# Turning the k product of a fused adaLN block from fp32 into three fp32r products

## The reference, cut to what matters

```python
x_prev = jnp.concatenate([jnp.zeros((B, 1, C), x.dtype), x[:, :-1, :]], axis=1)
xr = mu_r * x + (1.0 - mu_r) * x_prev
xk = mu_k * x + (1.0 - mu_k) * x_prev
r = jax.nn.sigmoid(jnp.einsum('btc,dc->btd', xr, W_r))
k = jnp.einsum('btc,dc->btd', xk, W_k)
k_act = jnp.square(jax.nn.relu(k))
out = r * jnp.einsum('btc,dc->btd', k_act, W_v)
```

## Time and profile before

| | |
|---|---|
| median of 3 runs | 732.72 us (731.6 to 733.01) |
| the profiled execution | 733.41 us |
| its span | 731.8 us, 11552 instructions |
| TensorE clock, mean granted | 0.979 |
| busy: TensorE, VectorE, ScalarE, GpSimd | 679.8, 524.3, 392.5, 387.3 us |
| the k product (L1274 into `work`) | 236 records of 592 ns, 106.2 us busy |
| the last product (L1108, L1109, L1110) | 78.1, 70.6, 70.7 us busy |

### The profile page before, as it was taken

One profiled execution on the slowest core, in us unless ns is written; L12 is line 12 of the kernel. 1 busy time (PEld: TensorE's weight loads), 2 busy tenths in 40 slices (PEclk: granted clock), 3 DMA queues, 4 the chain that ended last, 5 costly groups with the idle time before them and its releaser, 6 DMA issues. The chain is left out here.

```text
span 731.8 us, 11552 instructions
## 1 busy us (share of the span) xinstructions
PE 679.8 (93%) x3554; PEld 546.8 (75%) x3554; DVE 524.3 (72%) x1030; ACT 392.5 (54%) x871; POOL 387.3 (53%) x809
## 2 busy tenths in 40 slices
PE   5972999999999999999999999999999999998496
PEld 2751777888878777888878787888868787886475
DVE  4571699786877688786877688786877687477453
ACT  0330566554755656554755666555755566545453
POOL 4224487757635762757635762757535772255230
PEclk9996899999999999999999999999999999999899
DMA  8329536564764849463854848463854557424425
GB/s 300 102 75 239 162 123 153 93 146 121 161 135 74 205 86 208 79 152 106 180 114 78 202 93 201 85 154 98 183 111 79 115 99 166 86 61 84 58 29 87
DMA packets 90968, 93.02 MB, mean 127 GB/s; under 512 B 4216, under 2 KB 88992, under 8 KB 90944
## 3 DMA queue, kind: packets, MB, share of 16 engines
q0 software_dynamic: 33264, 33.03, 30.6%
q1 hardware_dynamic: 55600, 57.02, 24.9%
q10 hardware_dynamic: 2080, 2.68, 1.1%
HBM read 42.84 MB, written 33.10 MB: 104 GB/s over the span
## 5 line engine op out<-in xcount | busy, mean ns | idle before, releaser
L1224 PE MATMUL att<-m_sb,z_t 128*128 128x256 f32 x496 | 114.6, 385 | 19.9 <-issue 12.9
L1224 PEld LDWEIGHTS att<-m_sb,z_t 128*128 128x128 f32 x496 | 93.6, 192 | 37.0 <-issue 25.2
L1257 PE MATMUL work<-w_r_t,mx 128*128 128x256 f32 x464 | 105.2, 380 | 1.6 <-DVE mx L892 1.6
L1274 PE MATMUL work<-mx,w_k_t 128*128 128x512 f32 x236 | 106.2, 592 | 0.0
L863 DVE SCALAR_TENSOR_TENSOR t_buf<-att,rs_o,g_row 128x256 f32<-128x256 f32 x124 | 51.4, 477 | 65.7 <-POOL rs_o L467 65.6
L676 ACT ACTIVATE z<-x,ag 128x256 f32<-128x256 f32 x128 | 66.5, 597 | 56.0 <-POOL ag L460 56.0
L1257 PEld LDWEIGHTS work<-w_r_t,mx 128*128 128x128 f32 x464 | 85.9, 190 | 12.7 <-DVE mx L892 1.9
L629 ACT ACTIVATE sq<-att 128x256 f32<-128x256 f32 x124 | 46.0, 382 | 86.8 <-PE att L1224 86.8
L438 POOL TENSOR_TENSOR ag<-st 128x4 f32<-128x4 f32 x32 | 19.5, 610 | 134.6 <-DVE st L874 134.6
L1206 PE MATMUL gram<-z 128*128 128x256 f32 (+1 forms) x512 | 89.1, 327 | 0.0
L1206 PEld LDWEIGHTS gram<-z 128*128 128x128 f32 x512 | 79.8, 191 | 6.6
(11 more groups left out here) (169 smaller groups left out, 1362.1 us busy)
## 6 DMA issues: line engine op xcount, KB each, us to landing
x_in<-in_L_attn_x_dram SPq DMA_DIRECT2D x32, 512.0 KB, 5.3
x<-rows SPq DMA_DIRECT2D x32, 512.0 KB, 3.5
x<-in_L_attn_x_dram POOLq DMA_DIRECT2D x32, 512.0 KB, 9.4
out_dram<-x SPq DMA_DIRECT2D x31, 512.0 KB, 4.8
out_dram<-y POOLq DMA_DIRECT2D x29, 512.0 KB, 6.0
rows<-row_scratch SPq DMA_DIRECT2D x16, 128.0 KB, 3.5
rows<-row_scratch SPq DMA_DIRECT2D x8, 256.0 KB, 3.9
wqkv_sb<-in_L_attn_w_qkv_dram ACTq DMA_DIRECT2D x1, 1536.0 KB, 10.8
```

Source lines behind the costliest of these rows:

```text
L1224: ins = mm(att_banks(j, alone)[q][:, (t % 2) * D:(t % 2 + 1) * D], z_t[:, j, k, t * P:(t + 1) * P], m_sb[:, k], start=(k == 0), stop=(k == ...
L1257: ins = mm(r_banks(alone)[q][:, (t % 2) * D:(t % 2 + 1) * D], mixed(j, alone)[0][:, ch, tile], w_r_t[:, ch], start=(ch == 0), stop=(ch == ...
L1274: ins = mm(k_banks(alone)[dh][:], w_k_t[:, ch, rows_dh], mixed(j, alone)[1][:, ch], start=(ch == 0), stop=(ch == KD - 1))
```

## The change

`ffn_k` goes from one fp32 product to `mm3`, three fp32r products of high and low parts, with 512 columns each. The weights are kept as `w_k_hi` and `w_k_lo`: ScalarE's copy writes the high part, and `split_k` on VectorE the low part, once before row 0. For each chunk ScalarE copies `xk` into `xk_hi` (`split_xk`, 128x1024) and VectorE subtracts it from `xk` into `xk_lo` (`low_xk`, 128x1024). Both are single buffers and wait until the product before has been done. `ffn_k` waits for `xk_lo_ready` in place of `xk_mixed`, and `mix` waits for `xk_lo_ready` of the chunk before in place of `k_done`. `low_xk` of a chunk stands behind another operation on VectorE: behind `gate_o` of the chunk before for chunks 0 and 1, behind `stats_2` for chunk 2 and behind `stats_a` for chunk 3. The diff, cut:

```diff
@@ -92,7 +92,8 @@
         bv_col = sb("bv_col", [P, NP])
         wfc_c = sb("wfc_c", [P, NP, D])
         w_r_t = sb("w_r_t", [P, KD, D])
-        w_k_t = sb("w_k_t", [P, KD, D])
+        w_k_hi = part("w_k_hi", [P, KD, D])
+        w_k_lo = part("w_k_lo", [P, KD, D])
         w_v_t = sb("w_v_t", [P, KD, D])
         mu_col = sb("mu_col", [P, 2, KD])
         wv_t = sb("wv_t", [P, NP, D])
...
@@ -638,6 +643,12 @@
                     nc.scalar.activation(h2t[:, h, 1 + j * CT:1 + (j + 1) * CT], tr[h][:], ACT.Identity,
                                          bias=mod_now[:, h:h + 1], scale=mod_now[:, 2 + h:3 + h]).then_inc(h2_ready, 1)
+            def split_xk(b, j, alone=False):
+                i = CH * b + j
+                wait_past(act, k_done, 2 * i)
+                act.wait_ge(xk_mixed, i + 1)
+                nc.scalar.activation(xk_hi[:], mixed(j, alone)[1], ACT.Copy).then_inc(xk_hi_ready, 1)
+
             def take_r(b, j, alone=False):
                 i, y_j = CH * b + j, y_buf(j, alone)
...
@@ -681,6 +692,8 @@
                 n = b + 1
                 squares(b, 0)
+                if not first:
+                    split_xk(b - 1, 3)
                 copy_z_t(n, 0)
                 prep_base_qk(n)
                 if first:
...
@@ -696,6 +709,7 @@
                 copy_h2(b, 0)
                 squares(b, 2)
                 copy_z_t(n, 2)
+                split_xk(b, 0)
                 take_r(b, 0)
                 make_z2(b, 1)
                 take_k(b, 0)
...
@@ -703,11 +717,13 @@
                 squares(b, 3)
                 make_z2(b, 2)
                 copy_z_t(n, 3)
+                split_xk(b, 1)
                 copy_gram(n)
                 copy_gram_low(n)
                 copy_h2(b, 2)
                 take_r(b, 1)
                 take_k(b, 1)
+                split_xk(b, 2)
                 copy_gq(n)
                 make_z2(b, 3)
                 exps(n)
...
@@ -728,17 +745,21 @@
                 make_z2(b, 1)
                 squares(b, 3, alone=True)
                 copy_h2(b, 1)
+                split_xk(b, 0)
                 take_r(b, 0)
                 make_z2(b, 2)
                 take_k(b, 0, halves=(0,))
                 take_k(b, 0, halves=(1,))
+                split_xk(b, 1)
                 copy_h2(b, 2)
                 take_r(b, 1, alone=True)
                 make_z2(b, 3)
                 take_k(b, 1, alone=True)
+                split_xk(b, 2, alone=True)
                 copy_h2(b, 3)
                 take_r(b, 2, alone=True)
                 take_k(b, 2, alone=True)
+                split_xk(b, 3, alone=True)
                 take_r(b, 3, alone=True)
                 take_k(b, 3, alone=True)
...
@@ -755,7 +776,7 @@
             copy_gram_low(0)
             copy_gq(0)
             exps(0)
-            copy_weights(2, [(w_r_t[:], work[0]), (w_k_t[:], work[1]), (w_v_t[:], work[2])])
+            copy_weights(2, [(w_r_t[:], work[0]), (w_k_hi[:], work[1]), (w_v_t[:], work[2])])
             copy_pv(0)
             row_steps(0, True)
             with act.Fori(1, B - 1) as b:
...
@@ -879,7 +900,7 @@
                 i = CH * b + j
                 if not alone:
                     wait_past(dve, r_done, 2 * i - 2)
-                    wait_past(dve, k_done, 2 * i - 2)
+                    wait_past(dve, xk_lo_ready, i - 1)
                 wait_past(dve, xk_mixed, i)
                 dve.wait_ge(x2_ready, CH * b + (min(j + 2, CH) if made is None else made))
...
@@ -892,6 +913,12 @@
                         ins = nc.vector.scalar_tensor_tensor(dst[:, h], dif[:, h], mu_col[:, n, h:h + 1], prev[:, h],
                                                              ALU.mult, ALU.add)
                     ins.then_inc(ready, 1)
+
+            def low_xk(b, j, alone=False):
+                i = CH * b + j
+                dve.wait_ge(xk_hi_ready, i + 1)
+                wait_past(dve, k_done, 2 * i)
+                nc.vector.tensor_tensor(xk_lo[:], mixed(j, alone)[1], xk_hi[:].bitcast(F32), ALU.subtract).then_inc(xk_lo_ready, 1)
             def low_k(b, j, alone=False):
                 i = CH * b + j
...
@@ -951,6 +978,13 @@
                     ins = nc.vector.scalar_tensor_tensor(res[0:n, k], last_c[0:n], neg_d[0:n], res[0:n, k],
                                                          ALU.mult, ALU.add)
                 ins.then_inc(qk_ready, 1)
+
+            def split_k():
+
+                dve.wait_ge(w_copied, 4)
+                nc.vector.tensor_tensor(w_k_lo[:].rearrange("p k d -> p (k d)"), work[1][:],
+                                        w_k_hi[:].rearrange("p k d -> p (k d)").bitcast(F32),
+                                        ALU.subtract).then_inc(w_split, 1)
             def softmax_dif(b):
                 dve.wait_ge(score_done, b + 1)
...
@@ -1008,6 +1042,7 @@
                     prep_qk(n)
                 else:
                     gate_o(b - 1, 3)
+                low_xk(b, 0)
                 take_wvf(b)
                 make_x2(b, 2)
                 stats_2(b, 2)
...
@@ -1015,10 +1050,12 @@
                 make_z(n, 3)
                 mix(b, 1)
                 gate_o(b, 0)
+                low_xk(b, 1)
                 make_x2(b, 3)
                 mix(b, 2)
                 low_k(b, 1)
                 stats_2(b, 3)
+                low_xk(b, 2)
                 if far:
                     stats_a(n + 1, 0)
                 gate_o(b, 1)
...
@@ -1035,6 +1072,7 @@
                 mix(b, 3)
                 if far:
                     stats_a(n + 1, 3)
+                low_xk(b, 3)
                 gate_o(b, 2)
             def last_row(b):
...
@@ -1047,18 +1085,22 @@
                 make_x2(b, 2, mixes=0, alone=True)
                 mix(b, 0, made=3)
                 gate_o(b - 1, 3)
+                low_xk(b, 0)
                 stats_2(b, 2)
                 mix(b, 1, made=3)
                 make_x2(b, 3, mixes=2, alone=True)
                 take_wvf(b, alone=True)
                 low_k(b, 0)
+                low_xk(b, 1)
                 stats_2(b, 3)
                 mix(b, 2, alone=True)
                 gate_o(b, 0)
                 low_k(b, 1, alone=True)
+                low_xk(b, 2, alone=True)
                 mix(b, 3, alone=True)
                 gate_o(b, 1, alone=True)
                 low_k(b, 2, alone=True)
+                low_xk(b, 3, alone=True)
                 low_k(b, 3, alone=True)
                 gate_o(b, 2, alone=True)
                 gate_o(b, 3, alone=True, add=True)
...
@@ -1090,6 +1132,7 @@
             make_z(1, 0)
             make_z(1, 1)
             dve.wait_ge(mod_col_ready, 2)
+            split_k()
             dve.wait_ge(w_copied, 5)
             row_steps(0, True, True)
             with dve.Fori(1, B - 2) as b:
...
@@ -1261,7 +1304,7 @@
             def ffn_k(b, j, alone=False):
                 i = CH * b + j
-                pe.wait_ge(xk_mixed, i + 1)
+                pe.wait_ge(xk_lo_ready, i + 1)
                 for dh in range(KD):
                     if dh == 0 and not alone:
                         wait_past(pe, ro_ready, 2 * i)
...
@@ -1271,8 +1314,9 @@
                         pe.wait_ge(k_lo_ready, 2 * i - 1 + dh)
                     rows_dh = slice(dh * P, (dh + 1) * P)
                     for ch in range(KD):
-                        ins = mm(k_banks(alone)[dh][:], w_k_t[:, ch, rows_dh], mixed(j, alone)[1][:, ch],
-                                 start=(ch == 0), stop=(ch == KD - 1))
+                        ins = mm3(k_banks(alone)[dh][:],
+                                  (w_k_hi[:, ch, rows_dh], w_k_lo[:, ch, rows_dh], xk_hi[:, ch], xk_lo[:, ch]),
+                                  start=(ch == 0), stop=(ch == KD - 1))
                     ins.then_inc(k_done, 1)
             def ffn_out(b, j, alone=False):
...
@@ -1413,6 +1457,7 @@
             pe.wait_ge(fc_ready, 1)
             make_m(0)
             pe.wait_ge(w_copied, 5)
+            pe.wait_ge(w_split, 1)
             row_steps(0, True)
             with pe.Fori(1, B - 1) as b:
                 row_steps(b, False)
```

More of the change, by code:

```diff
@@ L148, in adaln_block @@
         xr, xk = mx[:, 0], mx[:, 1]
+        xk_hi, xk_lo = (part(n, [P, KD, CT]) for n in ("xk_hi", "xk_lo"))
         k_hi, k_lo = (part(n, [P, 2, KD, CT]) for n in ("k_hi", "k_lo"))
@@ L211, in adaln_block @@
         w_copied = sem("w_copied")
+        w_split = sem("w_split")
         row8_stored = sem("row8_stored")
@@ L265, in adaln_block @@
         xr_mixed = sem("xr_mixed")
+        xk_hi_ready = sem("xk_hi_ready")
+        xk_lo_ready = sem("xk_lo_ready")
         k_done = sem("k_done")
```

## The result

The changed kernel takes **740.4 us** (median of 4 runs, 739.43 to 741.02) against 732.35 us for the kernel before, run beside it (4 runs): ratio 1.0109, interval 1.0092 to 1.0127. It is 1.1% slower. 728.7 was forecast, and the range ended at 736.5.

The account below looks back on a forecast made before the run. The prediction took a steady row as bound by TensorE's program order with one wait, for `t_buf`. Six rows -8.4, row 0 0 and last row +4.3 gave -4.1, about 728.7 us from a 732.72 median; range 723.0 to 736.5.

Parts of the forecast that it names:

- The start: Before row 0, split_k's 0.7 us on VectorE lies hidden in 2.2 us of waiting for a row DMA: 0.
- the bodies: Steady rows from attention 2 to the next attention 0, with products 0, 1 and 2: 2.3 us shorter each.
- The product: Each chunk's k product: twelve passes at 0.216 us, 2.6 us in place of 3.44, 0.85 less.
- a rival (12%): Passes of the k product take 0.238 us: 0.27 less gain in each of 18 body products, 733.9 us, no change; 12%.
- More than 0.23 apart: Sign of being wrong: the k product's passes stand more than 0.23 us apart, where 0.216 was forecast.
- a cost of each instruction: Reading of the fp32r product's extra 0.011 us: 256 columns don't quite cover it, 512 do, hence 0.216 a pass.
- The seam: Steady rows from attention 0 to attention 2, with the row before's product 3: 0.9 us longer.
- three waits as described: Seam: VectorE stands some 2 us for ScalarE's copy, its 2.47 idle is used up, attention 2 waits 1.8 for t_buf.
- The fourth: Seam: TensorE waits 1.0 us for k_lo ahead of ffn_out(3).
- Row 0: The first row: chunk 1 comes 0.6 to 1.4 late, product 2 gives 0.85 back; net 0, ends -1 and +1.
- The last row: Row 7: +4.3 us; make_x2(0) 2.2 late, subtractions ahead of statistics +1.2 and +1.1, partly offset by shorter products.
- The rival on the slower side: The seam costs 2.2 us in ordinary rows too, by GpSimd stretched beside two-input VectorE operations: 736.5 us; 18%.

Follow-up runs that it names:

- e1: The changed kernel without TensorE's wait for the weights' low part (w_split) ahead of row 0: 735.59 us, ratio 1.0037.
- e5: The changed kernel with all its added VectorE and ScalarE work, but the k product left in fp32: 752.35 us, ratio 1.0256.
- e2: The changed kernel with chunk 3's subtraction low_xk behind gate_o of chunk 2 in the steady rows: 733.92 us, ratio 1.0012.
- e6: The kernel before with only the new fp32r product, fed by parts made once: 721.6 us, ratio 0.9831.
- e3: The changed kernel with ScalarE's copy split_xk of chunk 3 ahead of the next row's first squares, last row included: 738.0 us, ratio 1.006.
- e11: The changed kernel with only chunk 1's last-row subtraction moved, ahead of making x of chunk 3: 740.26 us, ratio 1.0094.
- e10: The changed kernel with split_k right behind softmax_norm(0), low_xk(b,3) behind gate_o, and both last-row subtractions moved into VectorE's idle places: 730.3 us, ratio 0.9929.
- e4: The changed kernel with the last row's subtractions of chunks 0 and 1 behind the statistics of chunks 2 and 3: 739.02 us, ratio 1.0084.
- e9: The changed kernel with the last row's subtractions of chunks 0 and 1 both behind the mix of chunk 1: 740.18 us, ratio 1.0086.

## Why the prediction was wrong

**The start: the step that failed.** "`split_k` (0.7) lies in 2.2 us of waiting for a row DMA: 0." I priced it in VectorE's queue and found it hidden there, which is true. I didn't ask who waits for it. The diff's last line has TensorE wait for it ahead of all of row 0, and VectorE reaches it only behind two chunks of the next row's normalization. The cost is 4.45 us (e1: gone with the line). With it added, -4.1 becomes about 0 and the sign is lost; 733.2 would still have been inside the range, and it took the bodies' 3.3 and the smaller terms below to leave it. The text costed the wait for the activations' low part wherever it stands, and this one nowhere.

**The product: right in kind, mis-sized.** 0.216 a pass was taken and 0.233 measured, near the 0.238 that I had as the bound and as a rival (12%). "More than 0.23 apart" was one of the signs of being wrong, and it came. The reading "a cost of each instruction" was a guess between two rows that could not tell; 0.119 at 256 columns fits a cost of each column as well. 1.75 a body in place of 2.3 is 3.3 us over six rows. The rival's sum, 733.9, is right about the steady rows (81.38 measured, 82.05 - 1.4 + 0.8 = 81.45 by it), but partly by luck: it takes 0.27 off product 0 as well, whose gain the prediction had already cut to 0.6, and has the seam 0.16 too short.

**The seam: right in length.** +0.9 was forecast, +1.06 measured, with three waits as described. The fourth, 1.0 ahead of `ffn_out(3)`, was 0.15: the prediction missed that the delay of `gate_o` also holds ScalarE (for `d_now`), so that the product's second half waits for the tanh. It cost nothing, because the wait for `t_buf` ends later. Experiment e5 puts all of it on the added work, and e2 most of it on the one subtraction ahead of `gate_o`. That TensorE's saving in the seam is worth nothing is shown by e6.

**Row 0: right as a net.** The work costs 1.44 there and the product brings 1.42 back.

**The last row: right.** +4.3 was forecast and +5.04 measured: 2.2 through the seam (2.19; e3 gives it back whole at `make_x2(0)`), and the two subtractions ahead of statistics. Of these e11 shows the second to be worth 1.13. The first was not separated, since each place that I tried for it met GpSimd's chain; 1.24 is what remains for it. The row as a whole varies by the place of the clock's low spell (95.8 in the change, 96.4 in e1), so that 5.04 lay so near 4.3 is in part luck.

**The rival on the slower side** had a mechanism, the collision of VectorE with GpSimd, that is real and decided three experiments, but it was not what made this change slower: in the changed kernel's seam VectorE stands idle just when GpSimd's `rstd_a` starts, and in the last row the first operation of `rstd_2(2)` and of `rstd_2(3)` takes 1.1 before and after.

The whole, by stretches: -4.1 forecast, 6.11 more at the start (4.45 for the wait, 1.66 for a later `m_sb`), 3.94 more in the steady rows (3.3 of it in the bodies, most of it the price of a pass, the rest the seam), 0.74 more in the last row and 0.09 less in row 0 make +6.6. Run e10 shows that the same product and the same added work can gain.

## What to carry to other kernels

For each operation that a change adds, read two lists: what it stands behind on its own engine, and every wait on the semaphore it raises, with all that is queued behind that wait. A one-time operation wants as much care as one in the loop: its 0.7 us cost 4.45, as much as six steady rows brought. Before a rate is taken from a row of another size, write both readings of it (cost per instruction, cost per element) and keep both in the sum. And when two engines can both be idle in a gap, put an added VectorE operation with two SBUF inputs where GpSimd is idle too, not right behind the operation that starts its chain.

## What I had not expected of the hardware

- fp32r records come 0.119 us apart at 256 columns and 0.233 at 512, at a granted clock of 1.00. An fp32 product of 512 columns shows as two records 0.43 apart. So twelve fp32r records cost 2.80 where eight of fp32 cost 3.44 in this product, 19% less.
- The first operation of GpSimd's chain, on four elements a partition, took 0.20 to 0.21 us alone, 1.11 beside one VectorE operation with two SBUF inputs of 1024 elements (e3), and 2.25 beside two of them in a row (e4). In both it ended within 0.1 us of VectorE's.
- The granted clock has a low spell near the last turn in every execution, and its place is worth some 1.4 us. In e1, e3, e9, e10 and e11 the clock was 0.66 to 0.72 in the 5 us behind the turn, and the part from there to the end took 31.0 to 31.5 us. In the change, e2 and e4, which have the same product, it was 1.00 there and the part took 29.6 to 29.8; it was 1.00 too in before, e5 and e6. An earlier turn isn't the cause by itself: e2 and e11 turn within 0.3 us of each other, and e1 has the change's last row. What sets it was not settled.
